# First half's recurrence levels among the second half's projections, second half's levels with the first half's outputs, centred values, and three stage seams redone

## The reference, cut to what matters

```python
xx = xshift - x
m = jnp.tanh((x + xx * time_maa_x) @ time_maa_w1)          # four small mixes, then
xw, xk, xv, xr = x + xx * (time_maa_{w,k,v,r} + m_{w,k,v,r} @ time_maa_w2)
r, k, v = xr @ W_r, xk @ W_k, xv @ W_v                      # 8 heads of 64
w = jnp.exp(-jnp.exp(time_decay + jnp.tanh(xw @ time_decay_w1) @ time_decay_w2))
def step(S, inputs):                                        # over the 64 tokens of a sequence
    kv = kt[..., :, None] * vt[..., None, :]
    y = jnp.einsum('bhi,bhij->bhj', rt, S + u[None, :, :, None] * kv)
    return (wt[..., :, None] * S + kv, y)
yn = ((y - mean) * jax.lax.rsqrt(var + LN_EPS)).reshape(b, t, c)   # mean, var over a head's 64 columns
return (yn * ln_w + ln_b) @ W_o
```

## Time and profile before

| | us |
|---|---|
| median of 3 runs | 1546.23 |
| lowest and highest | 1542.49, 1548.50 |
| the profiled execution | 1542.92 |
| its span, first to last instruction | 1541.1 |
| PE busy in it | 1416.0 (92%) |
| DVE busy | 1108.1 (72%) |
| ACT busy | 620.3 (40%) |
| POOL busy | 184.6 (12%) |

### The profile page before, as it was taken

How to read it: one execution, slowest core, us unless ns; L and a number is a source line. 1 busy time by engine, 2 the same in 40 slices (tenths; PEclk the granted TensorE clock), 3 DMA queues, 4 the chain that set the end, 5 groups by cost and what they waited for, 6 DMA issues and landing times. The chain is left out here.

```text
span 1541.1 us, 33235 instructions
## 1 busy us (share of the span) xinstructions
PE 1416.0 (92%) x13854; PEld 934.6 (61%) x13866; DVE 1108.1 (72%) x2268; ACT 620.3 (40%) x1288; POOL 184.6 (12%) x179
## 2 busy tenths in 40 slices
PE   9999999999999997999768999999989988978898
PEld 5677777777777775434455644444456555667454
DVE  5577777777887787770398787667668787565787
ACT  2555444554445442223103411110178886034643
POOL 3300000000000000130002000000000002153800
PEclk9999999999999999999989999999999999989999
DMA  6343444344455433400005200000045561040000
GB/s 256 138 168 129 147 149 152 131 148 154 162 181 172 136 106 118 143 1 0 2 7 223 110 1 0 0 0 0 0 160 206 192 230 38 0 167 2 1 28 28
DMA packets 55449, 153.65 MB, mean 100 GB/s; under 512 B 11997, under 2 KB 16861, under 8 KB 49162
## 3 DMA queue, kind: packets, MB, share of 16 engines
q1 hardware_dynamic: 50186, 134.82, 25.5%
q0 software_dynamic: 5120, 16.78, 2.8%
HBM read 117.73 MB, written 33.85 MB: 98 GB/s over the span
## 5 line engine op out<-in xcount | busy, mean ns | idle before, releaser
L804 ACT ACTIVATE l0x_prob<-l0x_prob,l0x_negmax 128x512 f32<-128x512 f32 x128 | 90.9, 712 | 114.3 <-DVE l0x_negmax L878 114.3
L649 PE MATMUL bank<-l0x_ctxT,l0x_upper_k 128*128 128x512 f32 x256 | 106.8, 417 | 1.3 <-PEq L272 1.3
L662 PE MATMUL bank<-l0x_upper_v,l0x_ctxT 128*128 128x512 f32 x256 | 106.2, 415 | 1.4 <-DVE l0x_V L857 1.4
L664 PE MATMUL bank<-l0x_upper_v,l0x_ctxT_lower 128*128 128x512 f32 x256 | 101.0, 394 | 0.0
L651 PE MATMUL bank<-l0x_ctxT,l0x_lower_k 128*128 128x512 f32 x256 | 100.8, 394 | 0.0
L663 PE MATMUL bank<-l0x_lower_v,l0x_ctxT 128*128 128x512 f32 x256 | 100.7, 393 | 0.0
L650 PE MATMUL bank<-l0x_ctxT_lower,l0x_upper_k 128*128 128x512 f32 x256 | 100.3, 392 | 0.0
L1228 DVE CUSTOM_DVE_ANT_0 l1x_prob<-bank,l1x_zeros 128x512 f32<-128x512 f32 x128 | 80.8, 687 | 15.4 <-PE bank L1094 15.2
L1179 ACT ACTIVATE l1x_prob<-l1x_prob,l1x_negmax 128x512 f32<-128x512 f32 x128 | 91.0, 715 | 0.0
L2011 ACT ACTIVATE f_silu<-bank 128x512 f32<-128x512 f32 (+1 forms) x24 | 13.5, 561 | 190.4 <-PE bank L1938 190.4
L607 POOL DMA_DIRECT2D turned_context<-l0x_whole x60 | 32.9, 548 | 473.7 <-ACT l0x_whole L782 473.7
(11 more groups left out here) (342 smaller groups left out, 3105.0 us busy)
## 6 DMA issues: line engine op xcount, KB each, us to landing
l0x_ctx<-in_ctx SPq DMA_DIRECT2D x16, 1024.0 KB, 5.1
turned_context<-l0x_whole POOLq DMA_DIRECT2D x64, 256.0 KB, 2.4
l1x_KT<-turned_context SPq DMA_DIRECT2D x16, 1024.0 KB, 7.5
l1x_ctx<-in_ctx SPq DMA_DIRECT2D x16, 1024.0 KB, 5.0
fp_weight<-l0x_weight_piece SPq DMA_DIRECT2D x24, 352.0 KB, 4.9
f_raw<-fp_weight SPq DMA_DIRECT2D x3, 2816.0 KB, 18.2
l0x_abs_piece<-in_L_ffn_w_gate SPq DMA_DIRECT2D x16, 512.0 KB, 4.8
l0x_abs_piece<-in_L_ffn_w_up SPq DMA_DIRECT2D x16, 512.0 KB, 5.4
```

What stands on the lines that cost most here:

```text
L649: nc.tensor.matmul(bank[:, :], w.upper_k[:, kc, cols], c, start=kc == 0, stop=False)
L662: nc.tensor.matmul(bank[:, :], c, w.upper_v[:, kc, :], start=kc == 0, stop=False)
L664: last = nc.tensor.matmul(bank[:, :], c_lower, w.upper_v[:, kc, :], start=False, stop=kc == CH - 1)
L804: nc.scalar.activation(w.prob[r][:, :], w.prob[r][:, :], ACT.Exp, scale=-1.0, bias=w.negmax[:, p:p + 1], accum_out=w.rowsum[:, b % 2, p:p ...
```

## The change

The end of the first attention: in the last batch DVE's work is reordered, one quantising slot is moved to the batch before, and the aggregates and the root of the first seven tiles' variance are taken here.

The opening of the time mix: only the last tile's moments are left. DVE normalises tiles 0 to 3, then the last moments, 4 and 5, then shifts, then 6 and 7. PE turns in the same order, with fewer fillers. low_decay(0) goes ahead of lora(1), decay(0) ahead of the mixes of j = 4.

Values: DVE centres each value tile over the 64 columns of a head as it empties its bank (`value`), in place of ACT's copy; `centre` in the recurrence is gone. (The mean over a head's columns of A times v is A times the mean of v.)

The levels: the seven levels of the first half go into time_mix, PE's blocks standing between the projections of the second half, DVE's takes and updates behind its mixes. The seven of the second half stand in wkv between outputs, turns and output products of tiles 0 to 3. The first half's AT lies on g.XNT, the halved decays on mixed[2]. Squares are ACT's, read from PSUM; normalising reads PSUM too.

The sparse blocks are joined: the scores of group 0 follow the key projection, the values use banks 4 to 7, and four units' `front` and two `sums` stand between DVE's value rows; the ternary loads are issued at the start of the joined block.

```diff
+            for level in range(LEVELS):              # time_mix, DVE, behind the mixes
+                for j in range(4):
+                    take(level, j)
+                if 1 <= level < LEVELS - 1:
+                    update(level)
+                if level >= LEVELS - 4:
+                    value(4 + level - (LEVELS - 4))
...
             low_decay(1)                              # time_mix, PE
-            for j in range(4, 8):
-                turned_out("k", 1, w.W_k, j)
+            turned_out("k", 1, w.W_k, 4)
+            products_of(0)
+            turned_out("k", 1, w.W_k, 5)
+            products_of(1)
+            turned_out("k", 1, w.W_k, 6)
+            turned_out("k", 1, w.W_k, 7)
+            products_of(2)
             decay(1)
-            for t in range(4, 8):
-                value(t)
-            for j in range(4, 8):
-                turned_out("r", 3, w.W_r, j)
+            value(4)
+            products_of(3)
+            value(5)
+            turned_out("r", 3, w.W_r, 4)
+            products_of(4)
+            value(6)
+            turned_out("r", 3, w.W_r, 5)
+            products_of(5)
+            value(7)
+            turned_out("r", 3, w.W_r, 6)
+            products_of(6)
+            turned_out("r", 3, w.W_r, 7)
...
+            products_of(0)                            # wkv, PE, second half
+            outputs(0)
+            outputs(1)
+            products_of(1)
+            outputs(2)
+            outputs(3)
+            pe.wait_ge(w.product_loaded["o"], 16)
+            products_of(2)
+            products_of(3)
+            turn(0)
+            turn(1)
+            out_product(0)
+            products_of(4)
+            turn(2)
+            out_product(1)
+            products_of(5)
+            turn(3)
+            out_product(2)
+            products_of(6)
+            out_product(3)
+            for t in range(4, TILES):
+                outputs(t)
+            turn(4)
...
+            behind = {1: [(variance, 0), (variance, 1)], 2: [(normalise, 0), (variance, 2), (normalise, 1)],
+                      3: [(variance, 3), (normalise, 2)], 4: [(normalise, 3), (add_out, 0)], 5: [(add_out, 1)],
+                      6: [(add_out, 2)]}
...
+FRONT_AT = {0: [1], 2: [2], 4: [3]}                  # sparse stage, DVE
+SUMS_AT = {2: [0], 4: [1]}
+            front(0)
             for t in range(TILES):
+                value_rows(t)
+                for v in SUMS_AT.get(t, []):
+                    sums(v)
+                for v in FRONT_AT.get(t, []):
+                    front(v)
```

More of the change, by code:

```diff
@@ L847, in _ @@
             sums_copy(LAST)
+            act.wait_ge(var_eps, 1)
+            nc.scalar.activation(g.rstd[:, 1, 0:TILES - 1], g.rstd[:, 0, 0:TILES - 1], ACT.Sqrt).then_inc(std_done, 1)
         @block.vector
@@ L1711, in _, with square @@
         def _(act):
+            def square(t):
+                act.wait_ge(y_full, t + 1)
+                nc.scalar.activation(w.AT[:, t, :], g.bank[t][:, :], ACT.Square).then_inc(squared, 1)
             def root(t):
@@ L2410, in _, with exponential @@
         def _(act):
+            def exponential(v):
+                act.wait_ge(shifted, v + 1)
+                nc.scalar.activation(prob(v)[:, :], prob(v)[:, :], ACT.Exp).then_inc(exp_done, 1)
             def heads_copy(group):
@@ L2423, in _ @@
                     heads_copy(v // 4 - 1)
[L2424 to L2426 removed]
+                if v + 1 < UNITS:
+                    exponential(v + 1)
         @block.vector
@@ new lines, in sums, with value_rows @@
+            def sums(v):
+                dve.wait_ge(exp_done, v + 1)
+                nc.vector.tensor_reduce(w.rowsum[(v + 2) % 4][:, :], blocks(prob(v)[:, :]), AX.X, ALU.add).then_inc(sum_done, 1)
+                dve.wait_ge(sum_done, v + 1)
+                nc.vector.reciprocal(w.rinv[v % 4][:, :], w.rowsum[(v + 2) % 4][:, :]).then_inc(rinv_done, 1)
+            def value_rows(t):
+                dve.wait_ge(full, 2 * 2 + t + 1)
+                for e in range(2):
+                    rows = slice(e * T, (e + 1) * T)
+                    for half in range(2):
+                        cols = slice(half * 256, (half + 1) * 256)
+                        ins = nc.vector.tensor_tensor(w.VB[half * T:(half + 1) * T, 2 * t + e, :], value_bank(t)[rows, cols],
+                                                      g.rows[rows, 2, cols], ALU.add)
+                ins.then_inc(taken, 1)
```

593 lines of the change are left out of this document (329 added, 264 removed).

## The result

The changed kernel takes 1521.85 us (median, 1519.6 to 1522.57) against 1545.6 us of the kernel before, timed beside it: a ratio of 0.9856, with an interval of 0.9828 to 0.9884. Timed again later, beside the last experiment, it took 1524.1 us, ratio 0.9874 (0.9852 to 0.9895). The prediction was 1522.7 us. The profiled execution took 1521.7 us with a span of 1519.9, so the two traces differ by 21.2 us where the sum said 23.5. The medians differ by 23.7.

The account below looks back on a forecast made before the run. PE and DVE were taken to bound the kernel in turns, the change making them overlap. The terms 0 - 2.2 + 14.7 - 29 - 7 gave -23.5 us, so 1522.7 us on the median's scale, range 1510 to 1537.

Parts of the forecast that it names:

- Part 1: Seam into the time mix: DVE's reordered last batch leaves the last rounding about where it was, 0 us (-1 to +1).
- Part 2: Time mix's opening and first projections: earlier shifts and fewer fillers -3.9, centring of value tiles 0 to 3 +1.7; -2.2 us.
- Part 3: First half's levels among the projections: seven blocks of 128 records at 2.1 us on PE, no issue idle, +14.7 us.
- rival A: Instruction supply: each of the seven blocks keeps 1.8 us and the sparse stage its wait; 1537 us, chance 0.13.
- Rivals C and D: C: blocks halve PE's clock over 15 projections, 1574, chance 0.04. D: DVE or ACT late, no overlap, 1540, chance 0.04.
- Part 4: From the second half's levels to the next stage: 102.3 us becomes 71.3, plus 2 for PE's clock, -29 us.
- the +2 for the clock: Recurrence: PE's lowered clock stays so for the first 25 us, +2 us (0 to +5) against the -31.
- Rival B: Recurrence: ACT's alternating Square and Sqrt need two table loads of 1.28 us a tile; +4, 1527 us, chance 0.07.
- Part 5: Joined sparse stage: first turn 5.0 us earlier and 2 us less from moving the ternary loads, -7 us.
- The turn's -5.0: Joined sparse stage: PE's first turn, until now held for scaled probabilities until 1357.1, comes at 1352.1, -5.0 us.
- The -2 for the stall: Sparse stage: ternary loads, issued beside PE's issue wait of 2.4 us, move under the projections, -2 us (0 to -5).
- Rival E: More than forecast: full clock in the opening (-2), nothing lost in the recurrence (-2), all the sparse stall (-3); 1515, chance 0.12.

Follow-up runs that it names:

- the last experiment: The changed kernel plus five fillers at the seam, both recurrence reorderings and the early first sparse turn with fillers: 1510.46 us, ratio 0.9785.
- the doubled blocks: The changed kernel with each of the first half's level products between the projections issued twice into the same bank: 1543.64 us, ratio 0.9996.
- alone: The kernel before with only its two sparse blocks replaced by the joined one: 1539.57 us, ratio 0.9968.

## Why the prediction was right, and where not

**Part 1**, 0 us: the end of the block hangs on SP's wait for the last store, as I said, in both kernels. The step that failed is that the last rounding stays where it was: the new order of DVE brings it 1.6 us closer to batch 14. The trace of before showed next to no idle time on DVE ahead of that rounding, and I should have read that. What I didn't think of is PE: its last output product now starts 3.9 us earlier (607.36 instead of 611.23) while the block's end stays, and its idle time grew from 1.73 to 5.62 us.

**Part 2**, opening: -3.9 predicted, -1.4 in the trace, and most of the missing part is the clock. The fillers at the seam bring 2.3 of the 2.5 us back and the first shift to the predicted 620.5. I had looked for the clock's dip where the trace of before showed it (it came, 0.50 from 636 to 642, the key product 5.22 us) and not where the change would make a new one. Centring: +1.7 predicted, 1.8 in the trace, 1.9 by experiment. Part 1 and 2 together were -2.2 and are about -1.2, with the executions' jitter on top.

**Part 3**: +14.7 predicted, +15.4 measured; overlap shown (25.3 us when undone), no supply stop (rival A false). That the price of issue was 0 was right; that projections with "few instructions in much time" protect it fits too, with the limit that the doubled blocks found: one line, not two. DVE's slack ahead of level 0 was 17.5 us (16 predicted). Rivals C and D are false: clock 1.00, no PE wait.

**Part 4**: -29 predicted, -31.5 measured. The chain of steps was 71.3 us and took 70.8. But inside it errors cancelled. Level 3's block began 19.2 us behind the first, 1.0 sooner than the 20.2 of the sum (the 5.03 us that PE waited for DVE ahead of it were in the sum), and took 3.69 us instead of 2.1 at half clock, 1.6 more. Outputs 4 to 7 took 3.95 us where I had 5.7, as no stop came behind the eight large records; the turns of tiles 4 and 5 waited 2.0. The failed term is the +2 for the clock on top of the chain: the clock did cost about that at level 3, and the shorter terms paid for it. The last weight landed some 2 us ahead of the next stage (3 predicted), and in no kernel did that stage's first turn wait for one. Rival B is false: one table load in the whole stage, for Square, Sqrt and the copies together.

```profile
773.61 1.28 ACT L1900 ACT_TABLE_LOAD   x1
```

That agrees with the Trainium skill, "ScalarE: Activation LUTs", section Table sets, as far as these three functions go.

**Part 5**: -7 predicted, -5.1, -3.0 (alone) and -3.1 (second trace) measured. The turn's -5.0 was -4.1: DVE worked without a gap and its value rows ran on to 1336.65. The -2 for the stall is the failed term: the one issue wait that remains (1.16 us) is 1.2 smaller than the 2.38 before, and behind the first turn the clock decides over 2 us.

Rival E had named the opening's full clock and nothing lost in Part 4; the first needed the fillers, the second came true by half.

## What to carry to other kernels

When one engine waits while another works through a stage, put the waiting engine's next work between the other's products: here some 30 us of vector work vanished behind 61 us of projections, for 15 us of matmuls between them. Blocks of many tiny matmuls are best kept to 128 records, with a few microseconds of large products between them: seven such blocks had no stop, and each of the seven doubled ones had one of 0.8 to 1.6 us. And whenever a change moves the end of an engine's work ahead of a barrier or a wait, ask how long PE then idles: behind the waits of 4.5 to 5.6 us here it ran at half clock for several us, and five discarded matmuls in the idle time (2.3 us of gain) were worth more than the 1.6 us that the reordering had brought against the kernel before. And when a wait is called issue, look whether another engine's result came just ahead of its end: level 3's block at the recurrence's start waited for DVE both times, and the row said so only once.

## What the runs showed of the hardware that I had not expected

Stops of PE's instruction supply lie 254 or 255 matmul records apart where blocks are long and products lie between, and 128 where small matmuls follow each other without them, level products or outputs; each costs 0.4 to 1.9 us, and once 2.8, in the outputs of the kernel before. Issue waits that don't lie at such a distance (1.78 us ahead of level 2, 111 records behind the last stop) end with DVE's update.

Idle times of PE of 1.3 us (fillers at the seam) and 1.75 us (old order in the last batch) left its next records at full speed (turns of rows at 0.55 us a record), and 2.5 us left a level block at 2.12. Idle times of 4.5 to 5.6 us were followed by slower records in every trace: 1.0 us a record at the seam, 3.4 to 3.7 us for level 3's block, 1.09 us for the first sparse turn instead of 0.6, with windows of 0.50 behind all three in the changed kernel. So were the waits of 3.1 to 3.6 us that come one after another where the levels stand behind the projections (0.60 over their 40 us). Half clock also came without any idle time, in the mixes with 32 input rows (0.50 from 636 to 642, PE busy 6.00 of 6.00), and the fillers at the seam, some 20 us ahead of them, didn't prevent it. Executions of the same code differ by 2 to 2.6 us in a stage, by where the clock is down (behind the first sparse turn 0.89 in the three traces that took 2 us longer, 1.00 in the seven others); a gain of 2 us at one place is read better from a stage's length in several traces than from the median.
